# First of 32 passes of a fused Mamba-2 decoder layer: one convolution unit and one transpose brought forward on TensorE; a clamp, an exponential and two weight remainders put behind a convolution

## What is computed

```python
proj = layernorm(x) @ in_proj_w.T            # gate 8192 | conv input 8192 + 2*1024 | dt 128
xBC  = silu(causal_conv4(proj[conv part]) + conv_b)
hs, B, C = split(xBC)                        # 128 heads x 64; 8 groups x 128 states, twice
dt   = softplus(proj[dt part] + dt_bias); dA = dt * -exp(A_log)
cum  = cumsum(dA) within 32 tokens ...       # state space scan, written here as one block of 64
L    = exp(cum_i - cum_j) where i >= j
y    = ((C_i . B_j) * L * dt_j) @ hs + D * hs
g    = y * silu(gate);  g = g * rsqrt(mean of g*g over each group) * norm_w
x    = x + g @ out_w.T
```

## Time and profile before

| | |
|---|---|
| median of 3 runs | 2863.83 us (2861.97 to 2866.99) |
| the profiled execution, own time | 2870.87 us |
| its span | 2869.1 us |
| TensorE busy | 2828.2 us (99%) |
| VectorE busy | 1999.2 us (70%) |
| ScalarE busy | 1453.9 us (51%) |
| GpSimd busy | 1316.5 us (46%) |
| DMA | 578.30 MB, 202 GB/s over the span |
| granted TensorE clock, mean | 0.991 of full speed |

### The profile page before, as it was taken

How to read it: one execution, slowest core, us unless ns; L and a number is a source line. 1 busy time by engine, 2 the same in 40 slices (tenths; PEclk the granted TensorE clock), 3 DMA queues, 4 the chain that set the end, 5 groups by cost and what they waited for, 6 DMA issues and landing times.

```text
span 2869.1 us, 56835 instructions
## 1 busy us (share of the span) xinstructions
PE 2828.2 (99%) x22480; PEld 2288.3 (80%) x22480; DVE 1999.2 (70%) x3154; ACT 1453.9 (51%) x2185; POOL 1316.5 (46%) x832
## 2 busy tenths in 40 slices
PE   7999999999999999999999999999999999999998
PEld 5788888778788788887888888888887888878876
DVE  7777768887667667677666666677666576666667
ACT  5666566655445535445445454544445354454443
POOL 4767767775344333443342443433444334433423
PEclk9999999999999999999999999999999999999997
DMA  7788777878566555555565564565665555555630
GB/s 242 266 303 290 264 269 258 274 254 289 182 196 194 177 184 184 184 184 187 194 198 185 187 198 162 187 194 171 200 199 181 185 188 186 185 190 170 197 105 20
DMA packets 179431, 578.30 MB, mean 202 GB/s; under 512 B 25249, under 2 KB 31905, under 8 KB 171105
## 3 DMA queue, kind: packets, MB, share of 16 engines
q1 hardware_dynamic: 179168, 574.66, 60.9%
HBM read 460.29 MB, written 114.29 MB: 200 GB/s over the span
## 4 chain that ended last, share of the span: by engine, by line
PE 92%; DVE 5%; ACT 1%; issue 1%; POOL 0%; DMA 0%; DVEq 0%; SPq 0%; ACTq 0%; POOLq 0%
PE p_in L469 53%; PE p_out L469 24%; PE p_y L469 9%; PE p_in L557 4%; DVE cv L1318 1%; PE p_y L663 1%; DVE o_ring L1258 1%; DVE t_y L1367 1%; DVE g_f L1379 1%; ACT cv L861 0%; DVE cum L1280 0%; DVE decay L1350 0%; PE p_y L685 0%; PE p_y L634 0%; DVE cum L1272 0%
## 5 line engine op out<-in xcount | busy, mean ns | idle before, releaser
L469 PE MATMUL p_in<-xnb,w_ring 128*128 128x512 f32 x6864 | 1683.4, 398 | 0.9 <-DVE cv L1318 0.9
L469 PEld LDWEIGHTS p_in<-xnb,w_ring 128*128 128x128 f32 x6864 | 1263.7, 189 | 266.5 <-issue 1.6
L1318 DVE SCALAR_TENSOR_TENSOR cv<-p_in,cpar,cv 128x504 f32<-128x504 f32 x954 | 700.0, 734 | 469.3 <-ACT cv L861 445.8
L1730 POOL TENSOR_TENSOR g_lo<-g_f,g_hi 128x512 fp32r<-128x512 f32 x256 | 342.5, 1339 | 1202.5 <-ACT g_hi L861 1202.5
L469 PE MATMUL p_out<-o_ring,g_hi 128*128 128x512 f32 x2048 | 639.0, 393 | 1.1 <-POOL g_lo L1730 1.1
L861 ACT ACTIVATE cv<-p_in,cpar 128x512 f32<-128x512 f32 x318 | 246.4, 775 | 642.0 <-PE p_in L469 604.4
L469 PEld LDWEIGHTS p_out<-o_ring,g_hi 128*128 128x128 f32 x2048 | 379.6, 188 | 81.8 <-issue 1.3
L469 PE MATMUL p_out<-o_ring,g_lo 128*128 128x512 f32 x1024 | 400.0, 391 | 0.0
L1355 DVE TENSOR_TENSOR x_tok<-p_in,dts 128x512 f32<-128x512 f32 x256 | 176.5, 690 | 290.0 <-PE p_in L557 288.5
L861 ACT ACTIVATE x_t<-cv 128x512 f32<-128x512 f32 x256 | 160.9, 628 | 309.3 <-DVE t_y L1367 285.9
L1741 POOL TENSOR_TENSOR ss<-ss,g_sq 128x512 f32<-128x512 f32 x190 | 309.3, 1628 | 7.5
(11 more groups left out here) (259 smaller groups left out, 2298.9 us busy)
## 6 DMA issues: line engine op xcount, KB each, us to landing
w_ring<-ws_scr SPq DMA_DIRECT2D x432, 512.0 KB, 3.7
o_ring<-ows_scr SPq DMA_DIRECT2D x192, 512.0 KB, 4.6
ws_scr<-w_ring SPq DMA_DIRECT2D x144, 512.0 KB, 5.7
decay<-cum_scr SPq DMA_DIRECT2D x126, 512.0 KB, 6.8
raw_w<-wt SPq DMA_DIRECT2D x144, 256.0 KB, 5.0
ows_scr<-o_ring SPq DMA_DIRECT2D x64, 512.0 KB, 6.0
raw_o<-owt SPq DMA_DIRECT2D x64, 256.5 KB, 5.3
acb<-x SPq DMA_DIRECT2D x3, 1024.0 KB, 7.2
```

What stands on the lines that cost most here:

```text
L469: return nc.tensor.matmul(o, lhsT=l, rhs=r, start=first, stop=last)
L1318: ins = V.scalar_tensor_tensor(acc[:, :, t:SEQ], src[:, :, 0:SEQ - t], cpar[:, 5 * m + 3 - t:5 * m + 4 - t], acc[:, :, t:SEQ], ALU.mult, A ...
L1730: T(g_lo[:, c % 2, :], g_f[:, c % 2, :], g_hi[:, c % 2, :].bitcast(F32), ALU.subtract).then_inc(glo_done, 1)
```

## The change

Only the pass n = 0 gets other instructions or another order; the later 31 passes are unaltered, and nothing is added or left out.

- TensorE: `to_tokens(1)` no longer follows unit 6; it stands inside it, behind its first four matmuls. Unit 8 (the chunk 3) stands ahead of `to_tokens(2)`, right behind unit 7, and no longer behind it.
- ScalarE: the exponential of the second half of the decay table, `exp(1)`, goes from the end of k = 3 to the end of k = 4, and the load of the Silu table behind it from k = 4 to k = 5.
- VectorE: `normal` goes from behind the convolution of chunk 3 to ahead of it. `clamped(1)` and the output remainders 2 and 3 (`refill_o(3)`) go from the end of k = 3 to k = 4, behind the convolution of chunk 4 and its `x_tokens`. `decayed(1)` goes from k = 4 to k = 5, behind the convolution of chunk 5.

```diff
-            def unit(k, tb, g, n):
+            def unit(k, tb, g, n, between=None):
...
                 for w, a in ((0, 0), (0, 1), (1, 0)):
+                    if a == 1 and between is not None:
+                        to_tokens(between, n)
...
-                    unit(6, tb, g, n)
-                    to_tokens(1, n)
+                    unit(6, tb, g, n, 1)
 
                 for k in range(2, CPG):
-                    if begun or k > 2:
+                    if begun or k > 3:
                         unit(2 + 2 * k, tb, g, n)
                     if k % 2 == 0:
                         heads(k - 2, tb, g, n)
                     unit(3 + 2 * k, tb, g, n)
+                    if k == 2 and not begun:
+                        unit(8, tb, g, n)
...
-                    if (k == 2 and (closing(tb, g) is not None or not begun)) or k == 3 or (k == 4 and (tb >= 1 and is_at(tb, g, 4) or not begun)) \
-                            or (k == 5 and former(opening(tb, g)) is not None):
+                    if (k == 2 and (closing(tb, g) is not None or not begun)) or k == 3 or (k == 4 and tb >= 1 and is_at(tb, g, 4)) \
+                            or (k == 5 and (former(opening(tb, g)) is not None or not begun)):
                         silu_table()
...
-                    if k == (2 if begun else 3):
+                    if k == (2 if begun else 4):
                         exp(1, n)
...
                 for k in range(1 if begun else 2, CPG):
+                    if k == 3 and not begun:
+                        normal(QT, xt[:, :], xt[:, :], QT)
                     conv(2 + k, n)
...
                     if k == 3 and not begun:
-                        normal(QT, xt[:, :], xt[:, :], QT)
                         decayed_half(1)
-                    if k == (3 if begun else 4):
+                    if k == (3 if begun else 5):
                         decayed(1, n)
                     x_tokens(k, n)
...
+                    if k == 4 and not begun:
+                        clamped(1, n)
+                        refill_o(3)
                     if k != 3:
                         refill_o(k)
...
-                    if k == 3 and not begun:
-                        clamped(1, n)
                     if k in (2, 3):
                         spread(k, tb, g)
-                    if k == 3:
+                    if k == 3 and begun:
                         refill_o(k)
```

## The result

The changed kernel took 2879.74 us as the median of 6 runs (2877.57 to 2881.67), the kernel before 2864.76 us (2861.97 to 2867.79, 6 runs): 15.0 us more, a ratio of 1.0049 with a 95% interval of 1.0038 to 1.0060. It is slower, as forecast, but by more: 2873.6 was forecast, and the range ended at 2878.5. The profiled execution took 2877.57 us, 6.7 more than the profiled one of before.

What follows compares the result with a forecast made beforehand. PE was taken as the bound, with idle time and low clock in the first pass. to_tokens(5) 7.7 us later plus 2.1 of low clock made 9.8, added to the median 2863.83: 2873.6, range 2865.0 to 2878.5.

Steps and rivals of the forecast that it cites:

- P: Start of to_tokens(4) behind project(1): taken as 78.7, the middle of 77.5 and 79.9, against 82.28 before.
- queue: SyncE's queue: raw unit 17 is issued 0.90 us after the second output remainder ends.
- landing of raw unit 17: The load of raw unit 17 lands 5.7 us after its issue; bounds 2.7 to 6.4.
- ScalarE to silu(5): From the split of unit 17 through output 4, table, exponential, tap0, convolution and silu: 8.0 us together.
- low clock behind it: PE behind the hole ahead of to_tokens(5): lower clock for a stretch, costing 2.1 us.
- rival 3: First pass: GpSimd's differences hold one product g_f, P is 79.9, 13.5 us slower with clock, 2877.3; chance 0.14.
- (d): Clamp, remainders, exponential and table load out of k = 3: the 2.59 us wait at to_tokens(4) and 1.6 low clock go.
- Rival 2: Same wait for raw unit 17, each piece near its least (clamp and remainders 2.7, landing 3): 2866.2; chance 0.18.
- (a): Chunk 1's transposes inside unit 6: heads start up to 1.6 us sooner, full clock gives another 1.6.
- (b): Unit 8 ahead of to_tokens(2) fills a wait under 1 us; unit 9 then needs x_tokens(2), at best 0.7 us.
- (c): normal ahead of chunk 3's convolution: PE's wait for the tile, about 1.3 us, goes, but nothing is gained.
- Rival 4: ScalarE's split of unit 17: load there by P + 0.9, early gains kept, faster at 2857.6 to 2858.8; chance 0.08.

Runs made afterwards that it cites:

- e2: The changed kernel measured and profiled once more, no edit: 2877.93 us, ratio 1.0045 to the kernel before.
- e12: The changed kernel with the first pass's output product of chunk 2 added five times, 48 more matmuls in the hole: 2872.88 us, ratio 1.0037.
- e3: The changed kernel with output remainders 2 and 3 back at the end of k = 3: 2862.27 us, ratio 0.9997.
- e6: The kernel before with only output remainders 2 and 3 moved to k = 4, behind x_tokens(4): 2879.0 us, ratio 1.0034.
- e9: e3 with GpSimd's differences of the second half between w_low of unit 13 and of unit 14: 2863.99 us, ratio 0.9991.
- e8: e3 with GpSimd's differences of the second half moved behind the first sum of squares: 2866.07 us, ratio 0.9999.
- e1: The kernel before measured and profiled once more, no edit: 2866.97 us, ratio 1.0004.
- e5: The kernel before with TensorE's part alone (to_tokens(1) inside unit 6, unit 8 ahead of to_tokens(2)): 2867.71 us, ratio 1.0004.
- e7: The kernel before with only normal, clamp, exponential, masking and Silu table moved; remainders and TensorE as before: 2864.05 us, ratio 0.9990.
- e10: The changed kernel with the first pass's output product of chunk 2 added four times, 36 more matmuls in the hole: 2877.22 us, ratio 1.0036.

## Why the prediction was wrong in its size

The mechanism is the one forecast, and each link of the chain behind to_tokens(4) came out close. Against the changed kernel's first profile:

| step of the prediction | forecast | measured |
|---|---|---|
| P: to_tokens(0) to (4) | 34.5 | 35.74, in e2 35.75 |
| transposes to the end of x_tokens(4) | 1.33 | 1.32 |
| clamp and two remainders | 5.67 | 5.39 (79.17 to 84.56) |
| queue | 0.90 | 0.89 |
| landing of raw unit 17 | 5.7 | 5.2 |
| ScalarE to silu(5) | 8.0 | 8.1 (90.67 to 98.77) |
| to_tokens(4) to (5) | 21.6 | 20.9, in e2 21.8 |
| hole ahead of to_tokens(5) | 12.7 | 12.05, in e2 12.95 |
| low clock behind it | 2.1 | 1.6 and 2.7 (e12 against the two profiles) |

e3 and e6 show the cause from both sides: taking the remainders back removes the hole, moving them alone makes it.

Between the first profiles of both kernels, the first pass grew from 92.07 to 101.90 us: 9.8, the very sum that was forecast. That is luck: two errors cancelled in it (P 1.2 later than I took it, the chain and the clock 1.2 shorter). By two profiles of each kernel the first pass grew by 11.4, by the medians the kernel by 15.0 and 12.2.

*P, the start of to_tokens(4).* I put it midway between 77.5 and 79.9, 34.5 us behind to_tokens(0). It came 35.74 and 35.75 us behind, which is rival 3's value (35.7). One product was held by the differences: 4.17 us. e9 shows that this was the reason: with the differences moved to where they hold neither product, P is 33.39 behind, the forecast's better end (77.5 less 44.18 is 33.3); e3, with the product held, has 35.73. The row of before had shown the same stall, and of two ends I should have taken the one that this row was nearest to. Rival 3 also named the rule of the Trainium skill (SBUF — State Buffer, "SBUF: two separate sides") by which one product is held; the trace agrees, 4.17 us beside the differences and 0.68 without them in e8. This is 1.2 us.

*The profile of before as the base.* The gain (d) counted 1.6 us of low clock behind the wait of 2.59. e1 has the same wait (2.57) and no low clock there: 9.16 us from mark (4) to (5) instead of 10.31. What I booked as won was in one of two profiles not there to be won: 1.1 us on the mark, 0.5 in the mean of the two.

*From one execution to the median.* I took the change of one execution and added it to the median of before, as if start and end were the same in all, and gave the range 1.2 us at either end for the scatter. The profiled execution of before stood 7.0 us above the median of 3 runs, that of the changed kernel 2.2 below its own (2877.57 against 2879.74). Of that difference 1.9 us are in the first twelve matmuls (last section). The unaltered kernel's own medians lay between 2863.63 and 2867.06 in the later sets, its single runs between 2858.8 and 2871.1. A term of 1.2 us was too small for this.

So two steps failed. In the sum it is P, which was sized 1.2 us too early because the stall of the product was left half out; with 0.5 for the base, and with chain and clock 0.2 shorter in the mean, that makes the 11.4 out of the 9.8. On top of the sum it is the carrying over to the median with 1.2 us for the scatter. The second set's 12.2 is near the 11.4, and its median, 2877.93, would have lain inside the range. In the first set the 15.0 lies 3.6 above, and the median of before was itself 0.9 above the base (2864.76 against 2863.83). Starts and ends of executions differ by more than 3.6 us, but that they make it up was not shown, and it stays open.

Two workings of the rivals were also wrong. Rival 2 read the earlier trace rows as one of 16 later clamps at 2.27 us: that one is the clamp at 72.28 itself, and the 15 behind it take 1.40 at most. In rival 3 the terms add up to 102.1 and not to 103, so its change would be 12.8 and not 13.5. The first touches neither forecast nor range, the second would have ended the range 0.6 us lower.

Of the others: (a) was right (heads 6.8 us behind to_tokens(0), as forecast, clock 1.00 from 50 to 60 us) and worth nothing, as e5 shows: what (b) called at best 0.7 us, the wait of unit 9, is 3.11. (c) fits the trace (no wait for the tile, but 1.33 us at the transposes behind it); no run tested it by itself. (d) was right in kind: the wait is gone, and e7, which moves all of it but the remainders, is the part that gains. Rival 2 fell, since the clamp took 1.99 and the remainders 3.48 beside a busy GpSimd. Rival 4 fell: raw unit 17 was there 12.7 us behind to_tokens(4), not 0.9.

## What to carry to other kernels

When an operation is moved later, look up whose semaphore wait in a DMA queue it releases, and what is queued behind that wait: here two remainders that nobody needed for 10 us released the load of something quite different, and the engine that waited for that load had the whole next chunk behind it. The stall of VectorE beside GpSimd's differences was not removed by moving them; it went to the next operation that met them (e8, e9). And a difference of some us is to be read between marks inside the traces, from two profiles of each kernel, since one execution's start, end and clock differ by as much.

## What the runs showed of the hardware that was not expected

**The start has two lengths.** The first twelve matmuls, the step sizes, take 3.02 to 3.04 us in 7 of the 14 profiles and 4.70 to 5.05 in the other 7, the same instructions in each, without idle time between them. In the first profiles of the changed kernel and of before:

```profile
14.62 3.03 PE L469 MATMUL p_y<-xnb,wd 128*128 128x512 f32 x12 [0.78 <-ACT xnb L864]
```

```profile
14.71 4.91 PE L469 MATMUL p_y<-xnb,wd 128*128 128x512 f32 x12 [0.78 <-ACT xnb L861]
```

The granted clock reads 1.00 in the windows from 14 to 18 us in both, so this column does not show it. Everything behind is about 2 us later: to_tokens(0) is at 41.8 to 43.2 us in the short ones and at 44.0 to 44.8 in the long ones. Both profiles of before were long, both of the changed kernel short. Which of the two an execution gets does not hang on the change: e10, which is the changed kernel in these twelve matmuls and far beyond, was long, and e6 and e7, in which TensorE has the order of before, were short. What makes the difference was not found.

**The end varies too.** From the last mean squares to the end of the span it is 75.7 to 76.8 us in nine of the profiles, 72.5 to 72.9 in three and 70.9 and 71.3 in two, whatever the kernel.

**The clock after a short hole.** It fell to the lower level behind holes of 4.43 us (e10) as behind 12, and behind the same wait of 2.6 us ahead of to_tokens(4) it fell in one profile of before and in e5 (units 12 and 13 in 7.35 and 7.33), but not in e1. Behind the wait of 3.11 us ahead of unit 9 the unit took 3.00 us in the first profile of the changed kernel and 4.22 in e2.
